# Expert blocks of 384 and 256 rows, rows normalized after the gather, and LayerNorm's pieces ahead of q's sum

## What is computed

```
h = layernorm(x) * (1 + ca) + sa
q, k, v = split(h @ w_qkv);  16 heads of 64
q = softmax(q * 0.125) over the head's 64;  k = softmax(k) over the 4096 rows
x = x + ga * ((q k^T as a 64 x 64 context per head, applied to v) @ w_out + b_out)
h = layernorm(x) * (1 + cb) + sb
p = softmax(h @ Wg + bg) over 8 experts;  the two best of a row, divided by their sum
x = x + gb * sum over the two experts e of p_e * (gelu(h @ W1[e] + b1[e]) @ W2[e] + b2[e])
```

## Time and profile before

| | |
|---|---|
| median of 3 runs | 865.39 us (865.19 to 865.96) |
| the profiled execution | 865.26 us, its span from first to last instruction 863.6 us |
| PE busy | 798.1 us, 92% |
| DVE, ACT, POOL busy | 575.3, 498.7, 327.3 us |
| mean granted TensorE clock | 0.965 of full |
| chain that ended last | PE 76%, DVE 11%, ACT 5% |

### The profile page before, as it was taken

How to read it: one execution, slowest core, us unless ns; L and a number is a source line. 1 busy time by engine, 2 the same in 40 slices (tenths; PEclk the granted TensorE clock), 3 DMA queues, 4 the chain that set the end, 5 groups by cost and what they waited for, 6 DMA issues and landing times.

```text
span 863.6 us, 18611 instructions
## 1 busy us (share of the span) xinstructions
PE 798.1 (92%) x6348; PEld 736.2 (85%) x6349; DVE 575.3 (67%) x1290; ACT 498.7 (58%) x979; POOL 327.3 (38%) x297
## 2 busy tenths in 40 slices
PE   5899999999998899844999999999999999999994
PEld 4677877888886689734999999999999999999994
DVE  6899999878888337793566655666556665665552
ACT  4556555666544413893856658566586565755552
POOL 2432331332321104002355544554445554555542
PEclk9999999999999999855999999999999999999998
DMA  8400000000001212544152522525325253232222
GB/s 293 129 1 2 1 1 2 2 2 2 1 2 49 99 63 74 173 116 168 25 146 45 141 47 39 146 41 143 46 40 146 40 144 45 43 49 49 41 48 24
DMA packets 45491, 57.59 MB, mean 67 GB/s; under 512 B 7810, under 2 KB 39236, under 8 KB 45316
## 3 DMA queue, kind: packets, MB, share of 16 engines
q0 software_dynamic: 14400, 20.24, 14.1%
q1 hardware_dynamic: 31044, 36.76, 12.7%
HBM read 38.24 MB, written 18.75 MB: 66 GB/s over the span
## 4 chain that ended last, share of the span: by engine, by line
PE 76%; DVE 11%; ACT 5%; issue 4%; DMA 1%; POOL 1%; SPq 0%; ACTq 0%; DVEq 0%; POOLq 0%
PE ps L1557 24%; PE ps L1545 23%; PE ps L1375 7%; PE ps L1333 7%; PE ps L1458 3%; PE ps L1396 3%; PE ps L1384 2%; PE ps L1528 2%; ACT at_lo L756 2%; DVE q_max L904 2%; DVE q_sum L911 1%; DVE k_blk L1014 1%; PE ps L1478 1%; ACT hid L811 1%; PE ps L1468 1%
## 5 line engine op out<-in xcount | busy, mean ns | idle before, releaser
L811 ACT ACTIVATE hid<-ps,b_col 128x256 f32<-128x256 f32 x296 | 122.4, 464 | 120.8 <-PE ps L1545 120.8
L1254 DVE TENSOR_TENSOR hid_lo<-hid,hid_hi 128x512 fp32r<-128x512 f32 x148 | 102.5, 692 | 113.2 <-ACT hid_hi L819 111.0
L1557 PE MATMUL ps<-w_hi,hid_hi 128*128 128x256 f32 x592 | 170.4, 288 | 2.3 <-DVE hid_lo L1254 2.3
L1545 PE MATMUL ps<-xT_hi,w_hi 128*128 128x256 f32 x592 | 167.8, 283 | 2.2 <-DVE xT_lo L1231 2.2
L1545 PE MATMUL ps<-xT_hi,w_lo 128*128 128x256 f32 x592 | 167.6, 283 | 0.0
L1545 PE MATMUL ps<-xT_lo,w_hi 128*128 128x256 f32 x592 | 167.5, 283 | 0.0
L1557 PE MATMUL ps<-w_hi,hid_lo 128*128 128x256 f32 x592 | 166.4, 281 | 0.0
L1557 PE MATMUL ps<-w_lo,hid_hi 128*128 128x256 f32 x592 | 166.4, 281 | 0.0
L588 POOL DMA_INDIRECT out<-y,y_id x74 | 132.5, 1791 | 53.3 <-DVE y L1263 41.9
L527 POOL TENSOR_TENSOR q_n<-q_exp,q_rec 128x1024 f32<-128x1024 f32 x32 | 61.9, 1934 | 170.7 <-DVE q_rec L912 170.7
L1545 PEld LDWEIGHTS ps<-xT_hi,w_hi 128*128 128x128 f32 x592 | 113.0, 191 | 2.6 <-issue 2.6
(11 more groups left out here) (201 smaller groups left out, 1418.0 us busy)
## 6 DMA issues: line engine op xcount, KB each, us to landing
w_raw<-in_L_ffn_W SPq DMA_DIRECT2D x16, 1024.0 KB, 7.4
x_all<-in_L_attn_x SPq DMA_DIRECT2D x8, 512.0 KB, 9.9
out<-x_all SPq DMA_DIRECT2D x8, 512.0 KB, 3.0
xrows<-x_all SPq DMA_DIRECT2D x8, 512.0 KB, 3.0
listed<-xrows,gid POOLq DMA_INDIRECT x76
out<-y,y_id POOLq DMA_INDIRECT x74, 3.9
wqk_raw<-in_L_attn_w_qkv SPq DMA_DIRECT2D x2, 512.0 KB, 6.9
wqk_raw<-in_L_attn_w_qkv SPq DMA_DIRECT2D x1, 1024.0 KB, 11.3
```

The costliest lines, as they stand in the source:

```text
L811: ins = act.activation(hid[:, m, :], ps[:, k, (m % 2) * BT:(m % 2 + 1) * BT], ACT.Gelu_apprx_tanh, bias=b1_col[:, bass.ds(e, 1), m])
L1254: dve.tensor_tensor(hid_lo[:, m, :], hid[:, m, :], hid_hi[:, m, :].bitcast(F32), ALU.subtract).then_inc(s_hid, 1)
L1545: last = pe.matmul(ps[:, k, (m % 2) * BT:(m % 2 + 1) * BT], w, a, start=st, stop=sp_)
L1557: last = pe.matmul(ps[:, Y0 + i, 0:D], a, w, start=m == 0 and st, stop=m == M - 1 and sp_)
```

## The change

1. **Blocks.** An expert's rows are counted in units of 128, at least 5; 6 is made 7. With an odd number of units it has one block of 384 rows, with an even one two, and the rest are blocks of 256 (`wide`, `narrow`). For the inputs above the units are 7, 9, 7, 9, 7, 10, 14 and 5, 68 in all (74 before): 10 blocks of 384 and 19 of 256, 29 together. Each engine has two loops per expert. Gather, transposes, `block_full` and `block_parts` work on 384 rows for every block; the products, gelu and scatters on the block's own size. A third accumulator takes bank 3, which the first product also uses, hence a new wait on s_y inside it.
2. **Weights.** All four parts of the next expert's weights are split in each wide block; the next load waits for the end of the wide blocks.
3. **Rows.** `normal` on ACT is gone. The stored row is x itself with 8 weights, the inverse deviation and the shift; DVE normalizes the gathered rows in `take` with three tensor_scalar instructions of 128x256, and `take` now stands before the last `hid_lo` of a block. `block_T` waits for it (s_norm) and not for the gather.
4. **Counting** is 11 short instructions (5 before) and stands behind the last one-hot; one more fills the end of `ids`.
5. **Stage 1.** `extra` and, from s = 3, `add_bias` of odd steps stand before `q_a`/`q_b`.

```diff
-BT = 256
+BT = 384
 BI = BT // P
 COLS = N // P
-ROW = D + E
-MAXB = N // BT
-MINB = 3
+META = E + 2
+ROW = D + META
+MAXB = 128
+UNITS = 5
 EPS = 1e-5
 SCALE = DH ** -0.5
...
             def store_rows(c):
 
-                sp.wait_ge(s_rown, (c + 1) * CH)
+                sp.wait_ge(s_x1, (c + 1) * CH)
...
             for i in range(BI):
                 sp.dma_start(xrows[N + i * P:N + (i + 1) * P, :], pad[:, i, :]).then_inc(s_xr, 16)
-            for c in range(GCH + 1):
+            for c in range(CHUNKS):
                 store_x1(c)
-            for c in range(GCH + 1, CHUNKS):
-                store_rows(c - GCH - 1)
-                store_x1(c)
-            store_rows(GCH - 1)
-            store_weights(0)
-            for c in range(GCH, CHUNKS):
                 store_rows(c)
+                if c == GCH + 2:
+                    store_weights(0)
             store_weights(1)
...
             for e in range(2, E):
-                sp.wait_ge(s_wlo, e)
+                sp.wait_ge(s_wfree, e - 1)
                 load_weights(e)
...
                     gv = now(pool, g)
-                    gather(e * COLS + b * BI + 2 * BI, gv + 2)
-                    scatter(e * COLS + b * BI, gv)
+                    gather(ahead(b + 2), gv + 2)
+                    scatter(pool.snap(to, min_val=0, max_val=E * COLS - 3), gv, 3)
+                    pool.reg_add(to, to, 3)
                     pool.reg_add(g, g, 1)
...
+                with pool.Fori(0, two) as b:
+                    gv = now(pool, g)
+                    gather(ahead(three + b + 2), gv + 2)
+                    scatter(pool.snap(to, min_val=0, max_val=E * COLS - 2), gv, 2)
+                    pool.reg_add(to, to, 2)
+                    pool.reg_add(g, g, 1)
...
-            def normal(c):
-
-                act.wait_ge(s_ln2, c // GCH + 1)
-                act.wait_ge(s_xo[c], 16)
-                for t in range(c * CH, (c + 1) * CH):
-                    act.activation(x_all[:, t, :], x_all[:, t, :], ACT.Identity, bias=bn_b[:, t:t + 1], scale=bn_r[:, t:t + 1]).then_inc(s_rown, 1)
...
+                    if parts:
                         act.wait_ge(s_wraw, e * 32 + 64)
+                        act.wait_ge(s_wlo, now(act, w) + ONE)
                         act.sem_inc(s_turn_act, 1)
-                    if parts:
-                        w_part(1 - par, parts[0])
+                        w_part(1 - par, 0)
                     block_full(gv + 1)
                     if parts:
-                        w_part(1 - par, parts[1])
+                        for n in range(1, 4):
+                            w_part(1 - par, n)
+                        act.reg_add(w, w, 1)
                     act.reg_add(g, g, 1)
 
-                rows_block(() if last else (0, 1))
-                rows_block(() if last else (2, 3))
-                with act.Fori(2, nb) as b:
-                    rows_block(())
+                with act.Fori(0, three) as b:
+                    rows_block(3, not last)
+                with act.Fori(0, two) as b:
+                    rows_block(2, False)
...
@@ -1034,6 +1044,9 @@
                 k_m(n)
                 if n == 0:
                     q_b(0, 2)
+                extra(n)
+                if j % 2 and s >= 3:
+                    add_bias((s - 3) * ST + j // 2)
                 s_, i = (s + 1, j // 2 - 1) if j >= 2 else (s, ST - 1)
                 if s_ < SBN:
                     if j % 2:
...
-                extra(n)
-                if j % 2 and s >= 3:
-                    add_bias((s - 3) * ST + j // 2)
                 if j % 2 == 0 and s >= 5:
                     add_bias(s * ST + j // 2)
...
                 link(dve.tensor_tensor(counts_f[:, :], list_next[:, :], list_start[:, :], ALU.subtract))
-                link(dve.tensor_scalar(counts_f[:, :], counts_f[:, :], float(BT - 1), None, ALU.add))
+                link(dve.tensor_scalar(counts_f[:, :], counts_f[:, :], float(P - 1), None, ALU.add))
                 link(dve.tensor_copy(counts[:, :], counts_f[:, :]))
-                link(dve.tensor_scalar(blocks[:, :], counts[:, :], BT.bit_length() - 1, None, ALU.arith_shift_right))
-                dve.tensor_scalar(blocks[:, :], blocks[:, :], MINB, None, ALU.max).then_inc(s_counts, 1)
+                link(dve.tensor_scalar(units[:, :], counts[:, :], P.bit_length() - 1, None, ALU.arith_shift_right))
+                link(dve.tensor_scalar(units[:, :], units[:, :], UNITS, None, ALU.max))
+                link(dve.tensor_scalar(parity[:, :], units[:, :], UNITS + 1, None, ALU.is_equal))
+                link(dve.tensor_tensor(units[:, :], units[:, :], parity[:, :], ALU.add))
+                link(dve.tensor_scalar(parity[:, :], units[:, :], 1, None, ALU.bitwise_and))
+                link(dve.tensor_scalar(wide[:, :], parity[:, :], -1, 2, ALU.mult, ALU.add))
+                link(dve.scalar_tensor_tensor(units[:, :], wide[:, :], -3.0, units[:, :], ALU.mult, ALU.add))
+                dve.tensor_scalar(narrow[:, :], units[:, :], 1, None, ALU.arith_shift_right).then_inc(s_counts, 1)
...
             hi_hot(2)
             place(1)
             hi_hot(3)
-            count_blocks()
             hi_hot(4)
             weigh(1)
             for c in range(GCH + 1, CHUNKS):
                 hi_hot(c)
+            count_blocks()
+            dve.tensor_scalar(ids[:, E * COLS:E * COLS + BI - 1], pad_row[:, E * COLS:E * COLS + BI - 1], float(N), None, ALU.add)
...
             def take(n):
 
-                dve.wait_ge(s_rows, n * 32 + 32)
+                dve.wait_ge(s_rows, n * 48 + 48)
                 dve.tensor_copy(y_next[:, :, :], listed[:, :, D:D + E]).then_inc(s_meta, 1)
+                for i in range(BI):
+                    last = dve.tensor_scalar(listed[:, i, 0:D], listed[:, i, 0:D], listed[:, i, D + E:D + E + 1],
+                                             listed[:, i, D + E + 1:D + E + 2], ALU.mult, ALU.add)
+                last.then_inc(s_norm, 1)
...
+                        if k == M // 2 - 1:
+                            take(gv + 1)
                         dve.wait_ge(s_hidhi, gv * 4 + (k + 1))
                         m = slice(2 * k, 2 * k + 2)
-                        dve.tensor_tensor(hid_lo[:, m, :], hid[:, m, :], hid_hi[:, m, :].bitcast(F32), ALU.subtract).then_inc(s_hid, 1)
-
-                    take(gv + 1)
+                        dve.tensor_tensor(hid_lo[:, m, 0:T], hid[:, m, 0:T], hid_hi[:, m, 0:T].bitcast(F32), ALU.subtract).then_inc(s_hid, 1)
+
                     block_parts(gv + 1)
-                    dve.wait_ge(s_added, gv * 32 + DMA2)
+                    if parts:
+                        w_low_part(0)
+                    dve.wait_ge(s_added, now(dve, u) * 16 + DMA3)
...
+                    for i in range(size):
+                        rows_out(i)
...
+                        w_low_part(1)
+                        w_low_part(2)
+                        w_low_part(3).then_inc(s_wlo, 1)
+                        dve.reg_add(w, w, 1)
...
+                with dve.Fori(0, three) as b:
+                    rows_block(3, not last_expert)
+                if not last_expert:
+                    dve.memset(tick[:, :], 0.0).then_inc(s_wfree, 1)
+                with dve.Fori(0, two) as b:
+                    rows_block(2, False)
...
-                pe.wait_ge(s_rows, n * 32 + 32)
+                pe.wait_ge(s_norm, n + 1)
                 for c in range(C):
                     for i in range(BI):
-                        last = pe.transpose(ps[:, XTB, c * BT + i * P:c * BT + (i + 1) * P], listed[:, i, c * P:(c + 1) * P], ident[:, :])
+                        last = pe.transpose(ps[:, XTB + c, i * P:(i + 1) * P], listed[:, i, c * P:(c + 1) * P], ident[:, :])
...
-                        if m % 2 == 0:
-                            pe.wait_ge(s_gelu, gv * 4 + (k + 1))
+                        if m == 0:
+                            pe.wait_ge(s_gelu, gv * 4 + FOUR)
+                        if size == 3 and m in (4, 6):
+                            pe.wait_ge(s_gelu, gv * 4 + (k - 1 + FOUR))
+                        if m == (3 if size == 3 else 6):
+                            pe.wait_ge(s_y, gv * 3 + THREE)
+                        to = ps[:, k, (m % 2) * T:(m % 2 + 1) * T] if size == 2 else ps[:, m % 4, 0:T]
                         col = slice(m * P, (m + 1) * P)
...
+                pe.wait_ge(s_wlo, now(pe, w) + 1)
+                pe.sem_inc(s_turn_pe, 1)
+                most, end = range(0, M - 2), range(M - 2, M)
+                with pe.Fori(0, three) as b:
+                    gv = now(pe, g)
+                    first(gv, 3)
+                    second(gv, 3, 0, most)
                     block_T(gv + 1)
-                    second(1, range(0, M - 2))
-                    second(0, range(M - 2, M))
-                    second(1, range(M - 2, M))
+                    second(gv, 3, 1, most)
+                    second(gv, 3, 0, end)
+                    second(gv, 3, 2, most)
```

(12 more changed lines are left out.)

197 lines of the change are left out of this document (99 added, 98 removed).

## The result

The changed kernel takes **850.85 us** (median of 4 runs, 849.50 to 851.49), the kernel before in the same session 865.67 us (4 runs, 865.19 to 867.05). The ratio is 0.9825, 95% interval 0.9809 to 0.9840: 15 us faster. The forecast was 847, 18 faster. The profiled execution took 851.43 us with a span of 849.6, where before it was 865.26 and 863.6.

A forecast was written before the change was run, and what follows sets the result against it. TensorE's instructions in a row were taken to bound the expert stage. Blocks -33.3, stalls +9.0, start +3.4, tail +1.9 and stage 1 +1.2 sum to -17.8 us against 865.26, giving 847 us, range 834 to 858.

The forecast's parts named there:

- Blocks, -33.3 + 9.0: Expert blocks: fewer, larger blocks save 33.3 us on TensorE, and waits for VectorE give back 9.0.
- a block of 256 rows costs what it did, and two more transposes: Narrow expert blocks on TensorE: 11.86 us as before plus 0.22 for two transposes, 12.08 us.
- ScalarE's table load, 0: Expert stage: the 1.28 us table load happens 3 times before and after the change, so it costs nothing.
- 384-wide matmul: First product of wide blocks on TensorE: 0.176 us per matmul, the middle between 256 and 512 columns; bounds 0.160 and 0.180.
- Six transposes: Start of an expert block on TensorE: transposes taken as 0.65 us in a wide block.
- Stalls, +9.0: Expert blocks: TensorE waits 0.2 us for `take` in 29 blocks, 5.8, plus 3.2 behind wide blocks' weight parts; bounds 0 to 18.
- Start, tail: Experts' start +3.4 us (third gather, `take`, transposes, eviction, later list copy); program's end +1.9 from a gather ahead of last scatters.
- Stage 1, +1.2: Stage 1 until 145 us: LayerNorm pieces stop stalling beside POOL, k_new stalls instead; +1.2 us, between -2 and +6.
- A: Rival, expert blocks: normalizing is hidden because tensor_scalar is faster than the one-hot; 838.4 us, chance 0.25.
- B: Rival, stage 1: k_new's delay reaches TensorE in full and isn't won back, +6 for +1.2; 852 us, chance 0.15.
- C: Rival, narrow blocks: POOL becomes the bound as VectorE's added instructions hold up descriptor writing; 871 us, chance 0.04.
- D: Rival, row counts: an expert near a multiple of 128 has a unit more, 5.9 us; 853 us, chance 0.01.

The follow-up runs named there:

- memset kernel: Changed kernel plus a useless 128x512 memset on POOL between list copy and first gather in 256-row blocks: 845.28 us, and 851.36 us on another chip.
- late_load: Changed kernel with TensorE's load of the number of narrow blocks moved behind an expert's wide loop: 842.26 us, ratio 0.9724.
- no_norm: Changed kernel without the three normalizing tensor_scalar instructions of each block, a short memset giving the semaphore instead: 844.32 us, ratio 0.9748.
- ln_back: Changed kernel with stage 1 in the old order, LayerNorm's pieces and odd steps' bias additions behind q's sum: 852.51 us, ratio 0.9847.
- pool_lag_again: Changed kernel with the useless 128x512 POOL memset ahead of narrow blocks' gathers, rerun beside the unchanged changed kernel on one chip: 851.36 us, ratio 0.9823.

## Why the forecast was right, and where not

- **Blocks, -33.3 + 9.0.** Too large by 5. The step that failed is "a block of 256 rows costs what it did, and two more transposes" with the gelus of the earlier trace rows beside it: I took the timeline of ScalarE and VectorE over unchanged and moved only the end of it, though I had put a third gather of POOL in the middle of the block myself and asked only whether POOL could keep up. The late semaphore costs 0.52 to 0.61 in ten blocks, 5.7 us: the memset kernel's narrow blocks inside an expert take 12.37 on the chip without the delay and 13.0 on one with it, and the whole kernel 6 us less.
- **A term that was missing:** the time of TensorE's own queue at the turn of an expert. It has two loads of counts and two loop entries where it had one of each; `late_load` gives 3.0 us back. I had costed it at nothing without naming it.
- **ScalarE's table load, 0.** At an outer turn it lengthened a block by 1.3 before (13.18 against 11.88) and 0.9 after (18.77 against 17.84), so it is a small gain.
- **What of the blocks was right:** 0.173 for a 384-wide matmul (0.176 taken; 0.160 and 0.180 were the bounds). The Trainium skill (TensorE: Matmul & The Clock Gate, Back-to-back issue gap) gives 162.5 ns for an isolated one by its formula; this stream's 173 is above it. Six transposes 0.71 (0.65). A wide block without turn or delay 17.7 (17.8), a narrow one 12.4 (12.3).
- **Stalls, +9.0.** PE waits 0.24 for `take` in a narrow block (0.2 taken), and the tensor_scalars are 0.32 apart (0.326 taken); `no_norm` puts all of normalizing at 7.2 us. Behind a wide block with weight parts a narrow one takes 12.43, against 12.37 behind a narrow one on the chip without the delay: 0.06 more, not 0.35, so some 2.6 of the 3.2 us weren't there.
- **Start, tail.** +3.1 and +2.3 for 3.4 and 1.9. The list copy came at 397.89 (398.2).
- **Stage 1, +1.2.** The stalls went where I said (k_new at 1.42 in most even steps up to 145 us, no LayerNorm instruction over 0.2), and the lag grew to 2.3 us; the later steps won more than I gave them, and the sum is -0.2, nothing that the scatter of the traces lets one tell from 0. The size was off, not the mechanism.
- **Rivals.** A falls (0.32 from start to start and 0.41 long, where the cast of this size is 0.29 long; 7.2 us for normalizing), and with it the two elements a cycle that the Trainium skill (VectorE: DVE Perf Modes, Mode 2×_2P) gives for such an instruction. B falls (`ln_back`). C falls as a bound: POOL idles 3.5 us a round. What it does to others by when it issues was on nobody's list. D falls: 232 gelus and 68 scatters, as counted.

The errors partly cancelled: 5.7 and 3 us not foreseen, and some 5 us of stalls, table loads and stage 1 foreseen too dear. So that 847 lies within 4 us of the measured time is in part luck: what was missed on either side is more than that.

## What to carry to other kernels

Moving or adding a DMA issue on an idle engine isn't free because that engine keeps up: look at which short waits of the critical chain fall right behind it. Price a turn of a loop on the engine that is the bound by its queue's own instructions (loads of trip counts, loop entries), and load what isn't needed yet later. Before a theory is built on a difference between kernels, run both on one chip: here one and the same kernel took 845.3 us on one chip and 851.4 on another, and the difference looked like the proof of a wrong theory until it was run again. And before a delay is put down to one of several things that come in a row, move that one alone.

## What the runs showed of the hardware

- On two of three chips a semaphore of TensorE came 0.55 us late in blocks in which POOL issued three indirect DMAs in a row, and moved by 0.4 when these were moved by 0.46; on the third the same program ran without it, 6 us faster (845.3 and 851.4). The traces with the delay lack more than half of the landing events of these DMAs, those without it under 1%.
- POOL's first indirect DMA starts 0.84 us behind the list copy that it needs; a memset of 128x512 in that gap moved it by only 0.05 (`pool_lag_again`).
- A two-pointer tensor_scalar of 128x256 in fp32 costs 0.32 us in a row of three, and a 384-wide fp32r matmul 0.173 in a stream, between the 0.120 of 256 columns and the 0.232 of 512.
